# A shorter quotient chain, masks made one at a time, residuals added as float32 transpositions, and new orders for every queue

## The reference

```python
x = x + L0_ffn(L0_cond(x, cond_8))   # LoRA; sparse attention and a sparse mixture of experts
x = x + L1_ffn(L1_cond(x, cond_8))   # one expert per batch; then the routing below, an FFN, a layer norm
x = x + L2_ffn(L2_cond(x, cond_8))   # chosen skills; then a soft mixture over 64 x 32 slots
x = x + L3_ffn(L3_cond(x, cond_8))   # one weight sum per batch; attention, shared FFN, routed experts
```

```python
scores = softmax(x @ wg + bg)                        # 16 experts
masked = scores * mask                               # the best 2 of 16 for each token
denom = masked.sum(0, keepdims=True) + 1e-6          # over the batches
route = masked / denom * 8
_, seq_ids = top_k(transpose(route), 128)            # for each expert and batch, half of the tokens
...                                                  # the chosen tokens go through an FFN, the others get 0
z = x + outs
return (z - z.mean(-1)) / sqrt(z.var(-1) + 1e-5) * gamma + beta
```

## Time and profile before

| | |
|---|---|
| median of 3 runs | 1142.11 us (1142.01 to 1143.24) |
| span of the profiled execution | 1140.3 us |
| PE | 1020.7 us busy, 90% of the span |
| DVE | 760.8 us busy, 67% |
| ACT | 499.1 us busy, 44% |
| POOL | 154.3 us busy, 14% |
| DMA | 35.39 MB, 31 GB/s on average |

### The profile page before, as it was taken

The page is one execution under the profiler, slowest core; times in us unless marked ns, Lnnn a source line. Parts: engine busy times, 40 slices in busy tenths (PEclk is TensorE's granted clock), DMA queues, the critical chain, the costliest instruction groups (busy, mean ns, idle before and its releaser), DMA issues.

```text
span 1140.3 us, 18292 instructions
## 1 busy us (share of the span) xinstructions
PE 1020.7 (90%) x6790; PEld 763.6 (67%) x6790; DVE 760.8 (67%) x1828; ACT 499.1 (44%) x823; POOL 154.3 (14%) x164
## 2 busy tenths in 40 slices
...
DMA packets 11800, 35.39 MB, mean 31 GB/s; under 512 B 2570, under 2 KB 5818, under 8 KB 10944
## 3 DMA queue, kind: packets, MB, share of 16 engines
...
...
## 4 chain that ended last, share of the span: by engine, by line
issue 42%; PE 41%; DVE 7%; POOLq 3%; ACT 3%; POOL 2%; DVEq 1%; ACTq 0%
PE ps L847 5%; PE ps L1147 5%; PE ps L1122 3%; PE ps L1298 3%; PE ps L1189 2%; PE ps L881 2%; PE ps L1209 2%; PE ps L857 2%; PE ps L1229 2%; PE ps L893 2%; PE ps L904 2%; POOLq L2153 1%; POOLq L2158 1%; PE ps L836 1%; DVE arena L1956 1%
## 5 line engine op out<-in xcount | busy, mean ns | idle before, releaser
L1975 DVE TENSOR_REDUCE arena<-ps 128x8 f32<-128x2048 f32 x32 | 73.2, 2288 | 27.1 <-PE ps L1189 27.0
L1506 ACT ACTIVATE arena<-ps 128x2048 f32<-128x2048 f32 x32 | 60.1, 1877 | 50.1 <-PE ps L1213 50.0
L1033 PE MATMUL ps<-arena,uR 128*128 128x512 f32 x128 | 68.8, 620 | 8.2 <-ACT arena L1451 7.9
L1122 PE MATMUL ps<-uR,arena 128*128 128x256 f32 x256 | 73.9, 385 | 0.0
L1058 PEld LDWEIGHTS ps<-arena 128*128 128x128 f32 x512 | 61.1, 191 | 6.6 <-issue 3.0
L1058 PE MATMUL ps<-arena 128*128 128x128 f32 x512 | 63.0, 276 | 2.0 <-DVE xacc L1898 1.2
L1298 PE MATMUL ps<-arena 128*128 128x512 f32 x128 | 61.7, 606 | 2.8 <-DVE xacc L2051 1.2
L1147 PE MATMUL ps<-arena 128*128 128x256 f32 x256 | 60.6, 384 | 3.2 <-DVE arena L1929 2.6
L1479 ACT ACTIVATE arena<-ps 128x512 f32<-128x512 f32 x64 | 37.8, 597 | 51.9 <-PE ps L1123 51.7
L847 PE MATMUL ps<-arena 128*128 128x256 f32 x256 | 58.3, 386 | 0.0
L1873 DVE TENSOR_REDUCE arena<-ps 128x16 f32<-128x512 f32 x64 | 44.3, 692 | 20.2 <-PE ps L1034 15.6
...
## 6 DMA issues: line engine op xcount, KB each, us to landing
...
```

Source lines behind the costliest of these rows:

```text
L1033: mm(high[:, c, :], uR[:, b, k * P:(k + 1) * P], phiC[:, col:col + 512], start=True, stop=False)
L1122: mm(o, phiC[:, st_ * P:(st_ + 1) * P], uR[:, b, :], start=True, stop=False)
L1506: av(pexp[:, t, gp].rearrange("p c h t -> p (c h t)"), scores[:, :, :].rearrange("p c t -> p (c t)"), ACT.Exp, scale=SCALE3).then_inc(s.sc ...
L1975: V.tensor_reduce(nm[:, k, :, 2 * gp:2 * gp + 2], scores[:, :, :].rearrange("p c (h t) -> p c h t", h=2), X, ALU.max, negate=True).then_in ...
```

## The change

- **Quotient.** The parts of the divisor, `dhi` and `dlo`, are made once at 128x32 and broadcast when they are used; the copy of the divisor to 128x256 and its split at that size go. Three temporary tiles instead of one take the products, so a product and a subtraction that don't depend on each other stand between two drains. The factor 8 moves from an instruction of its own into the copy of the transposed quotient out of PSUM (L1812).
- **Masks.** The mask of batch 0 is made in one instruction from the result of the rounds (compare and multiply); the 0/1 mask follows. The masks of batches 1 to 7 are steps MK.1 to MK.7 in DVE's list.
- **Residuals.** The identity matmuls in MOE, Z and WO get `is_transpose=True`: the same sum, by PE's transposition of float32 data.
- **Orders.** The lists of all engines in both stages are new (SP's of stage A excepted). In stage BD on POOL, W.0, W.1 and WA.1 stand ahead of RSZ.0, five W and WA steps between RSZ.1 and RSZ.2, four between RSZ.2 and RSZ.3, WA.6 behind RSZ.3, and W.7 and WA.7 behind JR1. On SP, EWA and EWB stand behind the last LOAD. On PE, DVE and ACT neighbouring steps change places.

```diff
 ORDER_BD = {
     "SP": """
-    LOAD.0 LOAD.1 LOAD.2 EWA.0 LOAD.3 LOAD.4 LOAD.5 LOAD.6 EWB.0 LOAD.7 EBD.0 ST.0 ST.1 ST.2 ST.3 ST.4 ST.5 ST.6 ST.7""",
+    LOAD.0 LOAD.1 LOAD.2 LOAD.3 LOAD.4 LOAD.5 LOAD.6 LOAD.7 EWA.0 EWB.0 EBD.0 ST.0 ST.1 ST.2 ST.3 ST.4 ST.5 ST.6
+    ST.7""",
     "PE": """
-    BC0.0 BC1.0 Z.0 ZT.0 BC0.1 SG0.0 BC1.1 SU0.0 Z.1 SG1.0 SU1.0 SG2.0 SU2.0 ZT.1 SG3.0 BC0.2 SU3.0 SG4.0 BC1.2 SU4.0
-    SU5.0 SG5.0 Z.2 UC.0 ZT.2 LG0.0 UT.0 LG1.0 BC0.3 MT0.0 SG0.1 SU0.1 MT1.0 SG1.1 SH0.0 SU1.1 SH1.0 SG2.1 SU2.1 LG2.0
...
+    BC0.0 BC1.0 Z.0 ZT.0 BC0.1 SG0.0 BC1.1 SU0.0 Z.1 SG1.0 SU1.0 SG2.0 SU2.0 SG3.0 ZT.1 SU3.0 SG4.0 BC0.2 SU4.0
+    BC1.2 SG5.0 SU5.0 Z.2 UC.0 ZT.2 LG0.0 UT.0 SG0.1 LG1.0 MT0.0 BC0.3 SG1.1 SU0.1 MT1.0 SH0.0 SG2.1 SH1.0 BC1.3
...
     "DVE": """
...
-    RM1.6 RM2.6 G3A.7 G3.7 FH0.7 FH1.7 FH2.7 RM3.6 FH3.7 RR.6 GE.7 RM0.7 Y2.7 RM1.7 RM2.7 FIN.6 RM3.7 RA.7 RR.7 OUT.6
-    FIN.7 OUT.7""",
+    BC0.0 MK.1 BC1.0 LN.0 ZN.0 X2.0 MK.2 BC0.1 BC1.1 SU0.0 LN.1 SU1.0 ZN.1 SU2.0 SU3.0 BC0.2 SU4.0 BC1.2 SU5.0 MK.3
+    LN.2 X2.1 MK.4 ZN.2 LG0.0 LG1.0 BC0.3 SU0.1 MK.5 MK.6 BC1.3 SU1.1 LG2.0 SU2.1 SH0.0 SU3.1 LG3.0 LG4.0 SU4.1
...
+    FH2.7 FH3.7 RM3.6 RR.6 GE.7 RM0.7 RM1.7 RM2.7 RM3.7 FIN.6 Y2.7 RA.7 RR.7 OUT.6 FIN.7 OUT.7""",
     "POOL": """
-    RSZ.0 RSZ.1 RSZ.2 RSZ.3 W.0 W.1 WA.1 W.2 WA.2 W.3 RSZ.4 WA.3 RSZ.5 W.4 RSZ.6 RSZ.7 WA.4 W.5 WA.5 W.6 WA.6 W.7
-    JR0.0 JR1.0 WA.7 VZ.0 CSA.1 CSB.1 QM.0 CSA.2 CSB.2 QM.1 RS1.0 QM.2 CSA.3 CSB.3 RS1.1 RS2.0 QM.3 CSA.4 CSB.4 RS1.2
...
+    W.0 W.1 WA.1 RSZ.0 RSZ.1 W.2 WA.2 W.3 WA.3 W.4 RSZ.2 WA.4 W.5 WA.5 W.6 RSZ.3 WA.6 RSZ.4 RSZ.5 RSZ.6 RSZ.7 JR0.0
+    JR1.0 W.7 WA.7 VZ.0 CSA.1 CSB.1 QM.0 CSA.2 CSB.2 QM.1 RS1.0 QM.2 CSA.3 CSB.3 RS1.1 RS2.0 QM.3 CSA.4 RS1.2 CSB.4
...
-                        last = mm(tail[:, k * P:(k + 1) * P], hsT[b % 3][:, k, :], ident, start=False, stop=k == K - 1)
+                        last = mm(tail[:, k * P:(k + 1) * P], hsT[b % 3][:, k, :], ident, start=False, stop=k == K - 1, is_transpose=True)
...
-                        last = mm(o, uR[:, b, k * P:(k + 1) * P], ident, start=False, stop=True)
+                        last = mm(o, uR[:, b, k * P:(k + 1) * P], ident, start=False, stop=True, is_transpose=True)
...
-                        mm(o, sC[u][:, k * P:(k + 1) * P], ident, start=True, stop=False)
+                        mm(o, sC[u][:, k * P:(k + 1) * P], ident, start=True, stop=False, is_transpose=True)
...
             V.reciprocal(rden, den)
+            V.tensor_scalar(dhi.bitcast(I32), den.bitcast(I32), -4096, None, ALU.bitwise_and)
             dr()
-            denw = den.unsqueeze(2).to_broadcast([P, K, NB, 16])
-            rdenw = rden.unsqueeze(2).to_broadcast([P, K, NB, 16])
+            wide_of = [P, K, NB, 16]
+            rdenw, dhiw, dlow = (a.unsqueeze(2).to_broadcast(wide_of) for a in (rden, dhi, dlo))
             V.tensor_tensor(route, msk[:, :, :, :], rdenw, ALU.mult)
-            V.tensor_copy(den_lo, denw)
+            V.tensor_tensor(dlo, den, dhi, ALU.subtract)
             dr()
             V.tensor_scalar(q_hi.bitcast(I32), route.bitcast(I32), -4096, None, ALU.bitwise_and)
-            V.tensor_scalar(den_hi.bitcast(I32), den_lo.bitcast(I32), -4096, None, ALU.bitwise_and)
             dr()
+            V.tensor_tensor(prod, q_hi, dhiw, ALU.mult)
             V.tensor_tensor(q_lo, route, q_hi, ALU.subtract)
-            V.tensor_tensor(den_lo, den_lo, den_hi, ALU.subtract)
-            V.tensor_tensor(prod, q_hi, den_hi, ALU.mult)
+            V.tensor_tensor(prod2, q_hi, dlow, ALU.mult)
             dr()
             V.tensor_tensor(rem, msk[:, :, :, :], prod, ALU.subtract)
-            for a, b in ((q_hi, den_lo), (q_lo, den_hi), (q_lo, den_lo)):
-                dr()
-                V.tensor_tensor(prod, a, b, ALU.mult)
-                dr()
-                V.tensor_tensor(rem, rem, prod, ALU.subtract)
+            V.tensor_tensor(prod3, q_lo, dhiw, ALU.mult)
+            dr()
+            V.tensor_tensor(rem, rem, prod2, ALU.subtract)
+            V.tensor_tensor(prod, q_lo, dlow, ALU.mult)
+            dr()
+            V.tensor_tensor(rem, rem, prod3, ALU.subtract)
+            dr()
+            V.tensor_tensor(rem, rem, prod, ALU.subtract)
             dr()
             V.tensor_tensor(rem, rem, rdenw, ALU.mult)
             dr()
             V.tensor_tensor(route, route, rem, ALU.add)
-            dr()
-            V.tensor_scalar(route, route, float(NB), None, ALU.mult)
             dr().then_inc(s.route_ready, 1)
             dve.wait_ge(s.route_T, 1)
-            V.tensor_copy(rR, PF[0][:, 0:T])
+            V.tensor_scalar(rR, PF[0][:, 0:T], float(NB), None, ALU.mult)
...
+            V.tensor_scalar(rRb[:, 0, :], rR, 0.0, con("rowb")[:, 0:1], ALU.is_lt, ALU.mult).then_inc(s.mask_ready, 1)
+            dr()
             V.tensor_scalar(rR, rR, 0.0, None, ALU.is_lt)
-            dr()
-            for b in range(NB):
-                V.tensor_scalar(rRb[:, b, :], rR, con("rowb")[:, b:b + 1], None, ALU.mult).then_inc(s.mask_ready, 1)
...
+                if n == "MK":
+                    V.tensor_scalar(rRb[:, b, :], rR, con("rowb")[:, b:b + 1], None, ALU.mult).then_inc(s.mask_ready, 1)
```

More of the change, by code:

```diff
@@ new lines @@
+    SU1.1 LG2.0 SU2.1 SG3.1 MT2.0 LG3.0 SH2.0 SG4.1 SU3.1 Z.3 LG4.0 MT3.0 SU4.1 SH3.0 MT4.0 SG5.1 SH4.0 SU5.1 LG5.0
+    LG6.0 UC.1 MT5.0 XT0.0 SH5.0 MT6.0 UT.1 SG0.2 XT1.0 SG1.2 LG7.0 SH6.0 SG2.2 ZT.3 MT7.0 SU0.2 SH7.0 LG0.1 BC0.4
+    SU1.2 MC.0 SG3.2 LG1.1 SG4.2 MT0.1 SU2.2 SG5.2 SH0.1 XT2.0 MT1.1 LG2.1 SU3.2 BC1.4 SH1.1 MT2.1 XT3.0 SH2.1 SU4.2
+    LG3.1 LG4.1 Z.4 MT3.1 SU5.2 MT4.1 SH3.1 SH4.1 LG5.1 UC.2 MT5.1 LG6.1 UT.2 SH5.1 XT0.1 MT6.1 SG0.3 LG7.1 ZT.4
+    SU0.3 SG1.3 SH6.1 XT1.1 SU1.3 SG2.3 MT7.1 LG0.2 SH7.1 SU2.3 SG3.3 LG1.2 SU3.3 MC.1 SG4.3 MT0.2 BC0.5 SH0.2 XT2.1
@@ new lines @@
+    MT1.2 BC1.5 LG2.2 XT3.1 SH1.2 MT2.2 SU4.3 SH2.2 LG3.2 LG4.2 SU5.3 MT3.2 SG5.3 Z.5 SH3.2 MT4.2 UC.3 LG5.2 SH4.2
+    XT0.2 LG6.2 MT5.2 SH5.2 UT.3 ZT.5 SG0.4 MT6.2 SU0.4 LG7.2 SH6.2 SG1.4 XT1.2 MT7.2 LG0.3 SH7.2 SU1.4 SG2.4 LG1.3
+    MC.2 SG3.4 MT0.3 SU2.4 SG4.4 BC0.6 SH0.3 XT2.2 SU3.4 MT1.3 SG5.4 BC1.6 SH1.3 LG2.3 LG3.3 SU4.4 MT2.3 Z.6 MT3.3
+    XT3.2 SH2.3 SH3.3 SU5.4 LG4.3 LG5.3 UC.4 MT4.3 XT0.3 MT5.3 SH4.3 SH5.3 UT.4 LG6.3 LG7.3 ZT.6 SG0.5 SU0.5 MT6.3
+    SG1.5 MT7.3 SH6.3 SH7.3 XT1.3 SU1.5 SG2.5 LG0.4 SG3.5 MC.3 SU2.5 SG4.5 LG1.4 BC0.7 MT0.4 SG5.5 SH0.4 SU3.5 XT2.3
@@ new lines @@
+    MT1.4 LG2.4 SH1.4 SU4.5 BC1.7 LG3.4 XT3.3 MT2.4 SU5.5 SH2.4 MT3.4 Z.7 LG4.4 SH3.4 UC.5 MT4.4 LG5.4 UT.5 SH4.4
+    XT0.4 MT5.4 LG6.4 SH5.4 SG0.6 LG7.4 SU0.6 MT6.4 SG1.6 SH6.4 ZT.7 MT7.4 XT1.4 SH7.4 SU1.6 SG2.6 LG0.5 MC.4 LG1.5
+    SG3.6 CL0.0 CL1.0 MT0.5 SU2.6 SG4.6 SH0.5 XT2.4 MT1.5 LG2.5 SU3.6 SH1.5 SG5.6 MT2.5 LG3.5 SH2.5 XT3.4 SU4.6
+    LG4.5 MT3.5 SH3.5 SU5.6 MT4.5 LG5.5 SH4.5 UC.6 MT5.5 XT0.5 LG6.5 SH5.5 UT.6 SG0.7 SU0.7 LG7.5 SG1.7 MT6.5 XT1.5
+    SH6.5 MT7.5 SG2.7 LG0.6 SH7.5 SU1.7 MC.5 LG1.6 SG3.7 SU2.7 SG4.7 MT0.6 SH0.6 XT2.5 MT1.6 LG2.6 SH1.6 SU3.7 LG3.6
@@ new lines @@
+    SG5.7 MT2.6 SU4.7 MT3.6 SH2.6 SH3.6 LG4.6 SU5.7 LG5.6 XT3.5 MT4.6 UC.7 SH4.6 XT0.6 LG6.6 MT5.6 SH5.6 XT1.6 MT6.6
+    SH6.6 LG7.6 CL2.0 CL3.0 UT.7 MT7.6 LG0.7 SH7.6 MC.6 LG1.7 MT0.7 CL4.0 SH0.7 CL5.0 LG2.7 XT2.6 MT1.7 MT2.7 SH1.7
+    CL6.0 SH2.7 LG3.7 XT3.6 LG4.7 MT3.7 SH3.7 CL7.0 MT4.7 SH4.7 LG5.7 LG6.7 CL0.1 CL1.1 MT5.7 XT0.7 SH5.7 CL2.1
+    LG7.7 MT6.7 XT1.7 CL3.1 CL4.1 MT7.7 SH6.7 SH7.7 CSP0.0 CL5.1 MC.7 CL6.1 XT2.7 CL7.1 XT3.7 CSP1.0 CSP2.0 JX0.0
+    CSP3.0 JM0.0 JX1.0 Y0.0 JM1.0 Y1.0 Y2.0 Y3.0 CL0.2 S.0 Q.0 V.0 CL1.2 K.0 CSUM.1 CL2.2 MX0.0 CL3.2 CL4.2 Y0.1
@@ new lines @@
+    XT1.6 MC.6 LG0.7 SH3.6 LG1.7 LG2.7 XT2.6 SH0.7 LG3.7 LG4.7 XT3.6 SH1.7 LG5.7 LG6.7 XT0.7 SH2.7 LG7.7 MC.7 XT1.7
+    SH3.7 JC0.0 XT2.7 JB0.0 XT3.7 JC1.0 JB1.0 REC.0 CN0.0 JA0.0 CN1.0 CN2.0 JA1.0 CN3.0 X3.0 CSUM.1 RQ.0 RK.0 REC.1
+    CN0.1 MX0.0 CN1.1 MX1.0 CN2.1 MX2.0 CN3.1 MX3.0 NM.0 X3.1 CSUM.2 RQ.1 RK.1 REC.2 CN0.2 MX0.1 SA0.0 CN1.2 SA1.0
+    MX1.1 CN2.2 MX2.1 X5.0 MX3.1 NM.1 CN3.2 FH0.0 G3A.0 G3.0 X3.2 FH1.0 RQ.2 FH2.0 FH3.0 Y2.0 GE.0 RK.2 MX0.2 MX1.2
+    SA0.1 RM0.0 MX2.2 SA1.1 MX3.2 NM.2 RM1.0 CSUM.3 X5.1 RM2.0 REC.3 CN0.3 G3A.1 CN1.3 CN2.3 RM3.0 CN3.3 RR.0 G3.1
```

209 lines of the change are left out of this document (92 added, 117 removed).

## The result

The changed kernel takes 1087.8 us (median of 4 runs, 1086.4 to 1090.7) against 1142.7 us for the kernel before on the same chip: a ratio of 0.9524, with a 95% interval of 0.9502 to 0.9546.

The account below looks back on a forecast made before the run. PE was taken as the bound in all layers, DVE's chain between the stages. Terms -1.3 - 1.8 - 4.8 - 4.8 - 0.6 + 2.0 = -11.3 us, from 1140.3 plus 1.8, gave 1131 us, range 1122 to 1140.

Parts of the forecast that it names:

- The quotient: Between the stages, DVE's chain from the reciprocal to the rounds gets shorter: 1.3 us saved (1.0 to 1.5).
- the masks: Between the rounds and DVE's first BC, batch 0's mask no longer waits for all eight: 1.8 us saved (1.4 to 2.0).
- The full clock at Z of batch 0: An earlier step Z may meet the lower clock for longer or shorter: 2 us either way, nothing in the sum.
- the residuals: In MOE, Z and WO, 48 transpositions each save 0.11 us of PE; 4.8 us saved (2.5 to 5.3).
- waits take the place of PE's gain: Rival: DVE or ACT is late next, only 5 of 9.6 us come through, near pairs cost 3.7: 1137 us; chance 0.14.
- the rounds don't stand still under POOL: Four POOL instructions beside the sixteen rounds don't hold up DVE: cost taken as 0, bounds 0 to 9.4 us.
- both rivals on the slow side: Rounds stand still under POOL (1140 us, chance 0.09); POOL holds DVE up at large, rounds included (1146 us, chance 0.09).
- batch 0's first LG cast would be held up: Four POOL steps behind RSZ.2 stall this cast and the difference behind it, so PE's MT0.0 waits: 2.0 us cost.
- the tail: FH3.7 ahead of RM3.6 takes a wait of 0.59 us from a DVE-bound chain: 0.6 us saved (0 to 1).
- the near pairs: Layers 1 and 2: ten more SH steps right behind their MT wait for ACT's copy: 2.0 us cost, up to 3.7.
- POOL's list: POOL's steps leave the middle of batch 0: 7.9 us saved, less new stalls; net 4.8 us saved (-7.9 to +3).
- Of the other pairs some are wider and some closer, in stage A as well: 0, with 3 us either way.: Remaining reordered PE pairs, beyond SH behind MT, were put at no net effect, with 3 us either way.

Follow-up runs that it names:

- e1: Kernel before with only the 48 identity matmuls of MOE, Z and WO as float32 transpositions: 1140.5 us, ratio 0.9989.
- e4: Kernel before with all new lists of both stages, without the MK steps; quotient, masks and residuals as before: 1098.9 us, ratio 0.9617.
- e3: Kernel before with POOL's new list of stage BD and nothing else: 1139.7 us, ratio 0.9972.
- e9: Changed kernel with the old order for the start of layer 3 only, up to batch 0's first routed expert: 1107.9 us, ratio 0.9705.
- e14: Kernel before with the new order at the start of layer 3 on PE, ACT and DVE, POOL's list old: 1128.7 us, ratio 0.9874.
- e10: Kernel before with two DVE steps moved one place (JA1.0 ahead of CN3.0, SA1.0 ahead of MX1.1): 1141.2 us, ratio 0.9995.
- e11: Kernel before with five PE steps moved one or two places, so five LG steps leave the SH they wait for: 1143.6 us, ratio 1.0010.
- e13: Kernel before with five steps of batches 1 and 2 moved at the start of layer 3, against DVE's waits at RQ.1 and RK.1: 1142.6 us, ratio 1.0016.
- e18: Kernel before with eleven steps moved at the start of layer 3: those of e13 and e10 and four more: 1136.3 us, ratio 0.9946.
- e7: Changed kernel with the old order of every step ahead of the start of layer 3 in stage BD: 1107.6 us, ratio 0.9688.
- e16: Kernel before with SH's wide dividing products on DVE left out, a tiny product in their place: 1134.2 us, ratio 0.9921.
- e5: Changed kernel with all old lists, the MK steps behind the same neighbours: 1136.3 us, ratio 0.9942.

## Why the prediction missed

**Right: the chain between the stages.** The quotient gave 1.47 us (1.3 forecast) and the masks 1.81 (1.8). The full clock at Z of batch 0, 0.9 us for its first eight matmuls, was in the range only.

**Right: the residuals, in this kernel.** 0.11 us each, also as a member of a sum, and 5.6 to 6.3 us in all for 4.8. The factor is two, as the lone transpositions of the earlier trace rows had it, not the four that the Trainium skill (TensorE: Matmul & The Clock Gate, terms table) states. With the old lists they brought only 1.3 to 1.8 us (e1). That is not the rival "waits take the place of PE's gain": up to the end of layer 2 3.4 of 3.5 us came through, and at the start of layer 3 PE's waits didn't grow, but its granted clock was lower. The prediction weighed the clock behind the rounds and behind POOL's stall, not there.

**Right: the rounds don't stand still under POOL.** POOL's four wide steps lie beside them (320.14 to 329.3 us; two of 2.36 and two of 1.91 us, where the forecast took 2.34 for all), and MAX8 takes 0.43 us with one or without. So both rivals on the slow side fell with their condition. The forecast that batch 0's first LG cast would be held up came true (first row), and cost PE one wait of 0.33 us, not 2.0; the worst cast of all 64 is now 1.37 us (second row: minimum, median, maximum), where the earlier trace rows had 2.07. A later one, beside WA.6, still takes 0.85 (395.79), over the 0.5 that was named as a sign of being right:

```profile
369.68 1.37 DVE L1879 CAST arena<-arena 128x16 bf16<-128x16 f32 x1
...
L1879 DVE CAST arena<-arena x64: 174/175/1373, 369.7 to 665.9; 128x16 bf16<-128x16 f32 x64
```

RSZ.2 came at 362.80, at once behind W.4, with DVE's statistics ready at 362.71: no delay, as costed. The half clock behind the old stall is gone; the granted clock is 1.00 from 350 to 420 us.

**Right in size, small: the tail and the near pairs.** From RM1.6 to the sum over the experts are 7.68 us (8.26 before): 0.6, as forecast, though not as it was argued. FH's wait for ACT didn't go, it is 0.91 us now, and RM3.6 waits 0.76 for PE; what fell is DVE's idle time in this piece as a whole, from 3.1 to 2.5 us. SH's wait for ACT's copy grew by 2.8 us (1.1 to 3.9), where 2.0 were put down.

**Wrong by a little: POOL's list.** -4.8 forecast, -2.7 alone. The stalls gave 6.4 as against 7.9, and 3.2 came back at the start of layer 3, where I had 0.7 for W.7 ahead of VZ and CSA.1: 1.5 of them by W.7, the rest with the lower clock.

**Wrong: "Of the other pairs some are wider and some closer, in stage A as well: 0, with 3 us either way."** This is the step that failed, and nearly the whole miss. All lists gave 43.4 us alone (e4), POOL's list by itself 2.7 (e3); the forecast had -3.4 for all of them (-4.8 + 2.0 - 0.6). Three things were wrong in it.

First, it priced only what the new order makes worse. It counted pairs that come closer (MT and SH) against the wait that they would cause, and, outside POOL's list, looked for no wait that would go. The same view of waits had 7.9 us at LG and 3.3 at SU in layers 1 and 2, both larger than the 1.1 that it did price; both are all but gone.

Second, it never looked at the start of layer 3 as a stretch. The earlier trace rows end at 700 and begin again at 820; "PE is the bound" was read from both sides of a gap in which PE was idle for 21.3 of 107.8 us. There the order of the steps was the bound, and e9 and e14 give 14 to 20 us for it.

Third, visible idle time understates the loss. A matmul that starts late by less than the latency of the one ahead leaves no idle time in the trace. From Z of batch 0 to JM0 I summed, for each matmul, the distance to the next start above the distance at which its kind follows itself: 50.0 us before, where the first table shows 29.4 us of idle time, 34.0 after, and 29.9 in the kernel with only the lists new. In front of LG these were 13.4 us before and 4.3 after, in front of MT 11.3 and 3.7, in front of SU 7.4 and 3.1, in front of SH 1.8 and 8.0. This is my working from the starts; matmuls at the lower clock count in it too, and lacking records raise it for the changed kernel.

**What the gain is.** Taking single waits away brought nothing, or at most 0.9 us (e10, e11, e13): each queue works in order, so a wait taken from one place is found again at the next step that another queue makes late. In e11 LG's waits fell by 3.9 us and those of SU and MT grew by 2.8; in e13 9.4 us of DVE's idle time became 4.5 for ACT, 3.1 and 4.6 for PE. With the next steps of PE and DVE moved too, the last of them was gone, and eleven moves together brought 6.5 us (e18), the whole order of that stretch 13.9 (e14), all lists 43.4 (e4). The reverse holds as well: in the new lists a part that is undone costs more than it gains alone (POOL's list 18.8 against 2.7, the start of layer 3 20 against 13.9; the clock has a share in the first). That single moves don't add up, and that the gain comes with further steps of PE and DVE, is thus shown for the start of layer 3; whether the four further moves would do alone is not. For layers 1 and 2 it is shown only that the lists ahead of JM are worth some 20 us (e7, e4), that PE's five pairs alone aren't the cause (e11), and that DVE's load is a part of it (e16).

**Open.** Which moves in layers 1 and 2 carry their 20 us isn't settled. New lists on PE, DVE or ACT alone, which would tell, weren't tried. How much of the 18.8 us of POOL's list comes from stalled DVE instructions, and how much from what the other queues expect of POOL, is open too. So is why the granted clock falls at the start of layer 3 in the traces of e1, e3, e5, e11 and e16 and not in that of before. None of the runs is faster than the changed kernel.
